# Plain float32 convolution for the first four tiles, and another order of the first steps

## The chip, the cores and the metric

The kernel runs on one NeuronCore of a Trainium2 chip. The metric is the device time of one execution in microseconds (us). The kernel before takes 187.44 us, the median of three runs (187.42 to 187.69).

The engines are named as the profile names them: PE is TensorE, PEld its weight load, DVE is VectorE, ACT is ScalarE, POOL is GpSimd and SP is SyncE, which here only issues transfers. SPq and ACTq are the instructions by which SP and ACT issue a transfer.

## The reference

```python
def cond(x, c, weight, c_weight, bias):          # x 128x32x512, 4 groups, 9 taps, padding 4
    out = lax.conv_general_dilated(x, weight, ..., feature_group_count=4)
    return out + einsum('nd,od->no', c, c_weight)[:, :, None] + bias[None, :, None]

def ffn(x, base_W, base_b, router_W, router_b, A, B, expert_map):   # x is cond's output
    base_out = x @ base_W.T + base_b                      # 512 -> 512
    probs = softmax(x @ router_W.T + router_b)            # 15 routes
    topk_p, topk_i = top_k(probs, 8)
    w = sum over k of topk_p * onehot(expert_map[topk_i]) # 8 experts
    h = einsum('btd,erd->bter', x, A)                     # 8 experts x 16
    lora = einsum('bter,eor->bto', h * w[..., None], B) * 2.0
    return base_out + lora

out = x + ffn(cond(x, ...))
```

## The kernel before, in words

**Tiles.** The 4096 rows (128 samples by 32 channels) of 512 positions are worked on as 32 tiles of 128 rows. A tile is 16 samples by the 8 channels of one convolution group. For each tile TensorE convolves (the positions are laid out in blocks so that a convolution is a product with 128x128 matrices, into `conv_banks`), VectorE adds the condition (`y_rows`) and transposes in 32x32 blocks (`y`), and TensorE multiplies `y` by one wide matrix, `wide_sb`, that holds A, the router and the base weights: 656 columns in two PSUM banks, the "front" bank of 400 columns and the "next" bank of 256, in four runs of 128 positions. From the front bank VectorE takes the router's scores, the eight best and the expert weights (`choose`, `best`, `mark`, `weigh`), and makes `hw`. TensorE turns `hw` (`turn_hw`) and multiplies it by B (`up`), into the same sums. VectorE adds them to the rows `xr`, and SP stores them.

**High and low parts.** A float32 operand is split in two float32r parts, a high one (ACT copies it with rounding: `wide_hi`, `y_hi`, `terms_hi`, `conv_hi`, `x_hi`, `hw_hi`) and a low one (the rest, by a subtraction on POOL or DVE: `..._lo`). Each product of the reference is then three float32r products: high by high, high by low, low by high.

**The first four tiles** are convolved from `x_in` directly: two matmuls (the group's own weights and those that reach into the next block) by three products, so six matmuls of 512 columns a tile, `conv_first` at line 566. Before them the input and the weights have to be split: `x_hi`, `x_lo`, `conv_hi`, `conv_lo`. Later tiles come from `terms`, prepared by an identity that saves a product: ACT copies one half of `terms` to PSUM (`odd_up`), DVE subtracts it (`difference`), ACT rounds (`terms_high`), POOL makes the rest (`terms_low`), and every second tile `edges` go through `edge`, `edge_high`, `edge_low`.

**Order.** There is no scheduler: each engine has its own program, written out by hand, and semaphores between them. TensorE starts with nine matmuls on zeros (`keep_warm`), convolves tiles 0 and 1, and then runs steps. Step t computes `linear(t)`'s front bank, `turn_hw(t-1)`, a part of the next bank, `up(t-1)`, the rest of the next bank, and the convolution of tile t+3. Steps 0 and 1 (`first_step`, `second_step`) have orders of their own, and convolve tiles 2 and 3. A step from 2 on starts when `y_lo` of its tile and the rows of tile t-2 (`out_added`) are there. `y_lo` is made by DVE for tiles 0 to 2 and by POOL from tile 3 on.

**Loads.** SP issues the transfers of the first tiles, of the wide matrix (four runs of 328 KB) and of most convolution weights, with a few waits between them; ACT issues the first two pieces of the convolution weights and the condition's inputs.

## Time and profile before

| what | us |
|---|---|
| median of three runs | 187.44 |
| profiled execution, its own time | 188.49 |
| profiled execution, span from first to last instruction | 186.7 |
| PE busy in the span | 180.1 (96%) |
| DVE busy | 156.2 (84%) |
| POOL busy | 143.9 (77%) |
| ACT busy | 82.9 (44%) |
| share of the chain that ended last on PE | 88% |

The mean granted TensorE clock is 0.997 of full speed. The profiled execution lies 1.05 us above the median, and 1.8 us of its time are outside the span. Share of the span says little of the first microseconds, where PE waits: the page's slices show PE at 7 and 8 tenths in the first three of 40 and 9 from then to the last. A line number names the line that records the instruction, which for the wide matmuls (L619), the convolution (L605, L566) and the subtractions (L217, L222) is a helper's.

### The profile page before, as it was taken

Reading aid. Unit: us, or ns where it says so; the run is one execution under the profiler, and the core shown is the slowest. Engines: PE = TensorE matmul, PEld = TensorE weight load, DVE = VectorE, ACT = ScalarE, POOL = GpSimd, SP = SyncE. Lnnn points to the kernel's source line nnn. Section 1 sums busy time; section 2 is a strip of 40 time slices with the busy share of each in tenths; the row PEclk is TensorE's granted clock in tenths of the full one; section 3 lists DMA queues with packets and bytes.
Section 4 is the critical chain, followed back from the end, with each engine's and each line's share of the span. In section 5 each row is a group of like instructions: output and inputs, shape, how many; then the busy total and the mean of one; then the engine's idle time right before and its main releaser. Section 6 shows DMA issues by size and latency. Waiting matters only on the chain.

```text
span 186.7 us, 3948 instructions
## 1 busy us (share of the span) xinstructions
PE 180.1 (96%) x1243; PEld 171.8 (92%) x1243; DVE 156.2 (84%) x513; ACT 82.9 (44%) x249; POOL 143.9 (77%) x141
## 2 busy tenths in 40 slices
PE   7889999999999999999999999999999999999992
PEld 2469979999999999999999999999999999999992
DVE  0997999989888888888888888889888889978673
ACT  3687344454343545444344545434354544422310
POOL 2639979988898888888988888879888887895410
PEclk9999999999999999999999999999999999999998
DMA  6999642755745454645555464754645631233313
GB/s 185 387 312 328 191 158 80 227 169 180 219 137 165 137 186 167 228 169 190 151 153 176 135 217 169 225 170 123 207 125 177 243 98 68 97 112 112 116 56 112
DMA packets 17733, 32.01 MB, mean 171 GB/s; under 512 B 1969, under 2 KB 2865, under 8 KB 17713
## 3 DMA queue, kind: packets, MB, share of 16 engines
q1 hardware_dynamic: 17136, 31.27, 51.9%
q10 hardware_dynamic: 576, 0.49, 0.9%
q8 instruction: 10, 0.16, 0.4%
q14 instruction: 11, 0.08, 0.1%
HBM read 23.36 MB, written 8.39 MB: 170 GB/s over the span
## 4 chain that ended last, share of the span: by engine, by line
PE 88%; DVE 4%; DMA 2%; issue 2%; ACT 2%; DVEq 0%; SPq 0%
PE wide_ps L619 58%; PE wide_ps L655 11%; PE conv_banks L605 10%; PE edge_bank L605 2%; DMA wide_sb<-wide_w 2%; PE odd_bank L642 2%; PE conv_banks L619 2%; PE conv_banks L566 2%; ACT wide_hi L350 1%; DVE xr L768 1%; DVE y_lo L887 1%; DVE y L859 0%; PE conv_banks L655 0%; DVE y_rows L774 0%; ACT y_hi L394 0%
## 5 line engine op out<-in xcount | busy, mean ns | idle before, releaser
L619 PE MATMUL wide_ps<-wide_hi,y_hi 128*128 128x400 f32 (+1 forms) x248 | 79.2, 325 | 1.3 <-ACT y_hi L394 0.7
L619 PE MATMUL wide_ps<-wide_hi,y_lo 128*128 128x400 f32 (+1 forms) x248 | 75.9, 312 | 0.0
L619 PE MATMUL wide_ps<-wide_lo,y_hi 128*128 128x400 f32 (+1 forms) x248 | 75.9, 312 | 0.0
L496 POOL TENSOR_TENSOR terms_lo<-terms,terms_hi 128x512 fp32r<-128x512 f32 x28 | 36.3, 1298 | 18.6 <-ACT terms_hi L379 18.5
L619 PEld LDWEIGHTS wide_ps<-wide_hi,y_hi 128*128 128x128 f32 x248 | 46.3, 188 | 3.9 <-ACT y_hi L394 1.1
L619 PEld LDWEIGHTS wide_ps<-wide_lo,y_hi 128*128 128x128 f32 x248 | 46.5, 189 | 0.0
L619 PEld LDWEIGHTS wide_ps<-wide_hi,y_lo 128*128 128x128 f32 x248 | 46.4, 188 | 0.0
L491 POOL TENSOR_TENSOR xr<-xr,base_b_sb 128x512 f32<-128x512 f32 x32 | 41.9, 1310 | 3.8 <-DMA xr<-x_rows 3.8
L514 POOL TENSOR_TENSOR y_lo<-y,y_hi 128x512 fp32r<-128x512 f32 x29 | 37.5, 1295 | 3.2 <-ACT y_hi L394 3.2
L401 ACT ACTIVATE hw_hi<-odd_bank 128x128 fp32r<-128x128 f32 x31 | 8.6, 277 | 52.7 <-PE odd_bank L642 52.7
L768 DVE TENSOR_TENSOR xr<-wide_ps,xr 128x512 f32<-128x512 f32 x30 | 20.7, 691 | 5.4 <-PE wide_ps L655 4.1
L859 DVE STREAM_TRANSPOSE y<-y_rows 128x512 f32<-128x512 f32 x32 | 22.8, 711 | 1.1
L394 ACT ACTIVATE y_hi<-y 128x512 fp32r<-128x512 f32 x32 | 20.0, 624 | 5.9 <-DVE y L859 4.9
L361 ACT ACTIVATE minus_best<-top 128x1 f32<-128x1 f32 x32 | 6.5, 203 | 32.6 <-DVE top L815 32.6
L379 ACT ACTIVATE terms_hi<-terms 128x512 fp32r<-128x512 f32 x28 | 17.3, 617 | 1.3 <-DVE terms L804 1.3
L605 PE MATMUL conv_banks<-terms_hi,conv_hi 128*128 128x256 f32 x56 | 15.7, 280 | 0.0
L605 PE MATMUL conv_banks<-terms_hi,conv_lo 128*128 128x256 f32 x56 | 15.7, 280 | 0.0
L605 PE MATMUL conv_banks<-terms_lo,conv_hi 128*128 128x256 f32 x56 | 15.6, 279 | 0.0
L842 DVE SCALAR_TENSOR_TENSOR hw<-wide_ps,inv,expert_w 128x128 f32<-128x128 f32 x31 | 10.9, 351 | 4.4
L655 PE MATMUL wide_ps<-up_hi,hw_lo 128*128 128x256 f32 x62 | 12.9, 286 | 0.0
L794 DVE TENSOR_TENSOR y_rows<-conv_banks,y_rows 128x256 f32<-128x256 f32 x28 | 11.9, 424 | 1.0
L797 DVE TENSOR_TENSOR y_rows<-edge_bank,y_rows 64x256 f32<-64x256 f32 x28 | 11.8, 422 | 1.0
(93 smaller groups left out, 321.3 us busy)
## 6 DMA issues: line engine op xcount, KB each, us to landing
xr<-x_rows SPq DMA_DIRECT2D x32, 256.0 KB, 3.6
out<-xr SPq DMA_DIRECT2D x31, 256.0 KB, 3.3
terms<-x_units SPq DMA_DIRECT2D x28, 256.0 KB, 3.0
edges<-x_edges SPq DMA_DIRECT2D x14, 256.0 KB, 3.5
wide_sb<-wide_w SPq DMA_DIRECT2D x4, 328.0 KB, 4.3
x_in<-x_first SPq DMA_DIRECT2D x4, 264.0 KB, 4.4
conv_sb<-conv_w SPq DMA_DIRECT2D x2, 192.0 KB, 5.0
conv_sb<-conv_w ACTq DMA_DIRECT2D x2, 128.0 KB, 4.5
```

The source lines that it names most:

```text
L379: nc.scalar.activation(terms_hi[i % 2][:, :, :, :], terms[i][:, :, :, :], ACT.Copy)\
L394: nc.scalar.activation(y_hi[k % 2][:, :, :], y[k % 2][:, :, :], ACT.Copy)\
L491: nc.gpsimd.tensor_tensor(xr[k][:, :], xr[k][:, :], base_b_sb[:, :], ALU.add)\
L496: nc.gpsimd.tensor_tensor(terms_lo[i % 2][:, :, :, :], terms[i][:, :, :, :], terms_hi[i % 2][:, :, :, :].bitcast(F32), ALU.subtract)\
L514: nc.gpsimd.tensor_tensor(y_lo[k % 2][:, :, :], y[k % 2][:, :, :], y_hi[k % 2][:, :, :].bitcast(F32), ALU.subtract)\
L605: mm = nc.tensor.matmul(sums, w[:, j, :], a[:, :, :], start=w is conv_hi and a is hi, stop=a is lo)
L619: mm = nc.tensor.matmul(sums_of(t, k)[:, b, 0:columns[1] - columns[0]], a[k % 2][:, r, :], w[:, r, columns[0]:columns[1]], start=r == 0 an ...
L655: mm = nc.tensor.matmul(sums_of(t, k)[:, b, first:first + HALF], a[k % 2][:, :], w[:, b * HALF:(b + 1) * HALF], start=False, stop=True, sk ...
L768: nc.vector.tensor_tensor(rows, linear_sums(t, k), rows, ALU.add)\
L794: nc.vector.tensor_tensor(rows[:, :, other, :], conv_ps[:, h, 1, :, :], rows[:, :, shared, :], ALU.add).then_inc(own_ready, 1)
L797: nc.vector.tensor_tensor(rows[reached, :, shared, :], edge_ps[reached], rows[reached, :, shared, :], ALU.add)\
L859: nc.vector.transpose(y[k % 2][:, :, :].rearrange("p r (n o) -> p n r o", n=Q), y_rows[k % 2][:, :, :, :].rearrange("p n a k -> p n (a k)"))\
```

## The change

The convolution of tiles 0 to 3 takes `x_in` and the loaded weights as they are, in float32, with two matmuls a tile instead of six. `x_hi` and `x_lo` are gone with their operations. The split convolution weights, used from tile 4 on, are kept in ten slots instead of fourteen, and the last pieces of them are split later (`conv_high(2)`, `conv_high(3)` in step 1). The condition's inputs and the convolution weights are one tensor, `conv_w`, loaded in pieces by columns. Tile 0's input is loaded and convolved in two halves. `y_hi` of tile 0 is made by DVE instead of ACT; `wide_lo` of run 0, `y_lo` of tile 2 and `up_lo` are made by POOL instead of DVE; the copies `cond_w_sb` by ACT instead of POOL. `up_lo` now reads a scaled copy `up_scaled`, made by ACT. The first `turn_hw` waits for the second `odd_up` instead of the first. The warm-up has six matmuls instead of nine. Steps 0 and 1 and the loads are in another order. The rest of the diff replaces `isinstance(t, int) and` by nothing, with the same program.

```diff
-WARM_UP = 9
+WARM_UP = 6
...
-            load_x(0)
+            for n, rows in enumerate(FIRST_ROWS):
+                load_first_x(n, rows)
+            load_x(1)
             load_wide(0)
-            load_x(1)
             load_wide(1)
-            sync.wait_ge(x_loaded[0], 16)
+            sync.wait_ge(x_first_in[1], 16)
             load_wide(2)
             load_wide(3)
             sync.wait_ge(wide_in[0], 16)
             load_conv(2)
             load_x(2)
             sync.wait_ge(wide_in[1], 16)
+            load_conv(3)
             load_x(3)
+            sync.wait_ge(wide_in[3], 16)
             load_terms(START, 0)
-            sync.wait_ge(wide_in[3], 16)
-            load_conv(3)
             load_edges(START // 2, 0)
...
+            act.wait_ge(cond_in, 16)
+            cond_weights(slice(0, 1))
+            cond_weights(slice(1, GROUPS))
+            bias_condition(range(1), 1)
             conv_high(0)
-            wide_high(range(1))
-            x_high(1)
-            bias_condition(0)
+            wide_high(range(RUNS))
+            bias_condition(range(1, 2), 2)
             conv_high(1)
-            wide_high(range(1, 2))
-            y_high(0, 0)
-            wide_high(range(2, RUNS))
-            conv_high(2)
-            x_high(2)
-            x_high(3)
+
+            y_high(1, 1, 2)
+            exponentials(0, 0)
+            bias_condition(range(2, GROUPS), 3)
             odd_up(START, 0)
-            y_high(1, 1)
-            conv_high(3)
-            bias_condition(1)
-            exponentials(0, 0)
             terms_high(START, 0)
             act.wait_ge(up_in, 16)
             nc.scalar.activation(up_hi[:, :], up_sb[:, :], ACT.Copy, scale=LORA_SCALE)\
                 .then_inc(up_hi_ready, 1)
+            nc.scalar.activation(up_scaled[:, :], up_sb[:, :], ACT.Copy, scale=LORA_SCALE)\
+                .then_inc(up_scaled_ready, 1)
             edge_high(START // 2, 0)
...
+            pool.wait_ge(wide_hi_ready, 1)
+            wide_low_part(nc.gpsimd, 0, wide_lo_first)
...
-            def conv_first_late(t):
-                pe.wait_ge(y_rows_ready, t - 1)
-                pe.wait_ge(conv_hi_ready, 3)
-                pe.wait_ge(x_hi_ready, t)
-                conv_first(t, (X_HIGH,))
-                pe.wait_ge(conv_lo_ready, 2)
-                conv_first(t, (X_W_REST,))
-                pe.wait_ge(x_lo_ready, t)
-                conv_first(t, (X_REST,)).then_inc(conv_done, 1)
+            def conv_first(t):
+
+
+
+                own, reach = t % 2, 1 - t % 2
+                nc.tensor.matmul(first_ps[:, t % 2, :, :], conv_sb[:, W_OWN[t], :],
+                                 x_in[t][:, :, own:own + BLK], start=True, stop=False)
+                nc.tensor.matmul(first_ps[:, t % 2, :, :], conv_sb[:, W_REACH[t], :],
+                                 x_in[t][:, :, reach:reach + BLK], start=False, stop=True)\
+                    .then_inc(conv_done, 1)
...
-                    pe.wait_ge(odd_ready, 1)
+                    pe.wait_ge(odd_ready, 2)
...
+            pe.wait_ge(conv_w_in[0], 16)
+            for n, rows in enumerate(FIRST_ROWS):
+                pe.wait_ge(x_first_in[n], 16)
+                for j, block in ((W_OWN[0], 0), (W_REACH[0], 1)):
+                    if n == 1 and block == 1:
+                        cond_sums(range(1), 1)
+                    mm = nc.tensor.matmul(first_ps[:, 0, rows, :], conv_sb[:, j, :],
+                                          x_in[0][:, rows, block:block + BLK],
+                                          start=j == W_OWN[0], stop=j == W_REACH[0])
+            mm.then_inc(conv_done, 1)
+            pe.wait_ge(conv_w_in[1], 16)
+            pe.wait_ge(x_loaded[1], 16)
+            conv_first(1)
+            cond_sums(range(1, 2), 2)
```

On POOL, the stretch from `terms_lo` of tile 4 (`terms_lo0<-terms0`, after the arrow what is read, with buffer numbers) to the split of the convolution weights reads before:

```order
L496 TENSOR_TENSOR terms_lo0<-terms0,terms_hi0 128x512 [waits terms_hi_ready]
L508 TENSOR_TENSOR edge_lo<-edges0,edge_hi 128x256 [waits edge_hi_ready]
L491 TENSOR_TENSOR xr0<-xr0,base_b_sb 128x512 [waits xr_loaded0,base_b_in]
L491 TENSOR_TENSOR xr1<-xr1,base_b_sb 128x512 [waits xr_loaded1]
L496 TENSOR_TENSOR terms_lo1<-terms1,terms_hi1 128x512 [waits terms_hi_ready]
L503 TENSOR_TENSOR edges1<-edges1 128x256 [waits edges_loaded1]
L514 TENSOR_TENSOR y_lo1<-y1,y_hi1 128x512 [waits y_hi_ready]
L222 TENSOR_TENSOR conv_lo<-conv_sb,conv_hi 128x384 [waits conv_hi_ready]
```

And now:

```order
L490 TENSOR_TENSOR terms_lo0<-terms0,terms_hi0 128x512 [waits terms_hi_ready]
L515 TENSOR_TENSOR up_lo<-up_scaled,up_hi 128x512 [waits up_hi_ready,up_scaled_ready]
L502 TENSOR_TENSOR edge_lo<-edges0,edge_hi 128x256 [waits edge_hi_ready]
L485 TENSOR_TENSOR xr0<-xr0,base_b_sb 128x512 [waits xr_loaded0,base_b_in]
L508 TENSOR_TENSOR y_lo0<-y0,y_hi0 128x512 [waits y_hi_ready]
L490 TENSOR_TENSOR terms_lo1<-terms1,terms_hi1 128x512 [waits terms_hi_ready]
L485 TENSOR_TENSOR xr1<-xr1,base_b_sb 128x512 [waits xr_loaded1]
L497 TENSOR_TENSOR edges1<-edges1 128x256 [waits edges_loaded1]
L508 TENSOR_TENSOR y_lo1<-y1,y_hi1 128x512 [waits y_hi_ready]
L479 TENSOR_TENSOR conv_lo<-weights_sb,conv_hi 128x256 [waits conv_hi_ready]
L479 TENSOR_TENSOR conv_lo<-weights_sb,conv_hi 128x384 [waits conv_hi_ready]
```

Three operations have come into the stretch (`up_lo`, `y_lo0` of tile 2, a `conv_lo` of 256 columns). Behind it both kernels go on alike: the rows of tile 2, `terms_lo` of tile 6, `edge_lo`, the rows of tile 3, and `y_lo` of tile 4.

On DVE, from the program's start to the weights of tile 0's experts (`hw0` follows the last row), before:

```order
L873 CAST x_hi0<-x_in0 128x528 [waits x_loaded0]
L222 TENSOR_TENSOR conv_lo<-conv_sb,conv_hi 128x256 [waits conv_hi_ready]
L217 TENSOR_TENSOR x_lo0<-x_in0,x_hi0 128x528 [waits x_hi_first]
L881 TENSOR_TENSOR wide_lo<-wide_sb,wide_hi 128x656 [waits wide_hi_ready]
L894 TENSOR_TENSOR is_expert<-cond_in_sb,expert_index 128x120 [waits index_ready,cond_in]
L774 TENSOR_TENSOR y_rows0<-conv_banks,cond_sb 128x512 [waits conv_done,cond_biased]
L859 STREAM_TRANSPOSE y0<-y_rows0 128x16x4x8 [waits y_rows_ready]
```

And now:

```order
L892 TENSOR_TENSOR is_expert<-weights_sb,expert_index 128x120 [waits index_ready,cond_in]
L779 TENSOR_TENSOR y_rows0<-conv_banks,cond_sb 128x512 [waits conv_done,cond_biased]
L864 STREAM_TRANSPOSE y0<-y_rows0 128x16x4x8 [waits y_rows_ready]
L900 CAST y_hi0<-y0 128x512 [waits y_ready]
L886 TENSOR_TENSOR y_lo0<-y0,y_hi0 128x512 [waits y_hi_first]
L226 TENSOR_TENSOR wide_lo<-wide_sb,wide_hi 128x656 [waits wide_hi_ready] x3
L779 TENSOR_TENSOR y_rows1<-conv_banks,cond_sb 128x512 [waits conv_done,cond_biased]
```

The splits of tile 0's input and of its weights are gone from in front of `y_rows0`, and the low parts of the wide matrix stand behind `y_lo0`. `difference` of tile 4 (`terms0<-terms0,odd_bank`) has moved too: it stood right behind the maximum of tile 0's scores, and stands now behind `hw0`.

On PE, from the first matmul after the warm-up to the first wide one, before:

```order
L566 MATMUL conv_banks<-x_hi0,conv_hi 128x512 [waits x_hi_first,conv_hi_ready]
L566 MATMUL conv_banks<-x_hi0,conv_hi 128x512
L566 MATMUL conv_banks<-x_hi0,conv_lo 128x512 [waits conv_lo_first]
L566 MATMUL conv_banks<-x_hi0,conv_lo 128x512
L628 MATMUL edge_bank<-cond_in_sb,cond_w_sb 128x128 [waits cond_w_ready,cond_in]
L628 MATMUL edge_bank<-cond_in_sb,cond_w_sb 128x128
L566 MATMUL conv_banks<-x_lo0,conv_hi 128x512 [waits x_lo_first]
```

And now:

```order
L666 MATMUL conv_banks<-x_in0,weights_sb 128x256 [waits x_first_in0,conv_w_in0]
L666 MATMUL conv_banks<-x_in0,weights_sb 128x256
L666 MATMUL conv_banks<-x_in0,weights_sb 128x256 [waits x_first_in1]
L624 MATMUL edge_bank<-weights_sb,cond_w_sb 128x128 [waits cond_in,cond_w_ready]
L666 MATMUL conv_banks<-x_in0,weights_sb 128x256
L566 MATMUL conv_banks<-x_in1,weights_sb 128x512 [waits x_loaded1,conv_w_in1]
L568 MATMUL conv_banks<-x_in1,weights_sb 128x512
L624 MATMUL edge_bank<-weights_sb,cond_w_sb 128x128 [waits cond_biased,cond_w_ready]
L609 MATMUL wide_ps0<-wide_hi,y_hi0 128x400 [waits wide_hi_ready,y_hi_first]
```

The first matmul waits only for transfers now, and not for DVE and ACT.

## Rows read from the trace of the kernel before

**Rows 1.** Stretches: busy time of each engine, PEclk, DMA share, GB/s.
```profile
30.00:170.00 140.00, 139.93 (x1009) 138.58 (x1010) 122.79 (x422) 62.34 (x195) 119.46 (x106) 1.00 0.51 163
```

**Rows 2.** Chain that ended last, 0 to 40 us: start, us, what.
```profile
14.82 0.45 PE edge_bank L628 x4
15.27 1.45 PE conv_banks L566 x6
...
20.33 0.12 PE odd_bank L642
...
24.05 2.42 PE wide_ps L619 x12
...
30.07 2.44 PE wide_ps L619 x12
...
35.97 2.19 PE wide_ps L619 x12
```

**Rows 3.** Timeline of PE: start, us, line, operation, [idle before, releaser].
```profile
0.99 3.88 PE L553 MATMUL wide_ps<-zeros 128*128 128x512 bf16 x9 [0.99 <-POOL zeros L459]
...
10.56 1.85 PE L619 MATMUL wide_ps<-wide_hi,y_hi 128*128 128x400 f32 x8 [0.67 <-ACT y_hi L394]
```

**Rows 4.** Timeline of DVE, first 18 us.
```profile
4.19 0.43 DVE L873 CAST x_hi<-x_in 128x528 fp32r<-128x528 f32 x1 [4.19 <-DMA x_in<-x_first]
...
6.11 1.08 DVE L881 TENSOR_TENSOR wide_lo<-wide_sb,wide_hi 128x656 fp32r<-128x656 f32 x1 [0.21 <-ACT wide_hi L350]
7.11 1.38 DVE L894 TENSOR_TENSOR is_expert<-cond_in_sb,expert_index 128x120 f32<-128x120 int32 x1
8.42 0.68 DVE L774 TENSOR_TENSOR y_rows<-conv_banks,cond_sb 128x512 f32<-128x512 f32 x1
9.13 0.71 DVE L859 STREAM_TRANSPOSE y<-y_rows 128x512 f32<-128x512 f32 x1
...
10.54 0.69 DVE L887 TENSOR_TENSOR y_lo<-y,y_hi 128x512 fp32r<-128x512 f32 x1
11.18 1.59 DVE L881 TENSOR_TENSOR wide_lo<-wide_sb,wide_hi 128x656 fp32r<-128x656 f32 x2
...
15.97 0.40 DVE L804 TENSOR_TENSOR terms<-terms,odd_bank 128x256 f32<-128x256 f32 x1
...
16.82 0.18 DVE L826 SCALAR_TENSOR_TENSOR wide_ps<-wide_ps,exps 128x15 f32<-128x15 f32 x1 [0.29 <-ACT exps L364]
...
17.75 0.35 DVE L842 SCALAR_TENSOR_TENSOR hw<-wide_ps,inv,expert_w 128x128 f32<-128x128 f32 x1
```

**Rows 5.** Groups by line, 0 to 32 us: shapes, count, busy us, mean ns, idle before.
```profile
L628 PE MATMUL edge_bank<-cond_in_sb,cond_w_sb 128*128 128x128 f32 x8 | 1.3, 284 | 0.2 <-POOL cond_w_sb L470 0.2
...
L605 PE MATMUL conv_banks<-terms_hi,conv_lo 128*128 128x256 f32 x4 | 1.1, 278 | 0.0
```

**Rows 6.** DMA, 0 to 25 us in 40 slices: GB/s moved.
```profile
GB/s 0 0 27 67 308 400 406 382 393 413 399 378 346 386 398 348 370 370 334 297 305 213 161 200 272 334 390 405 401 400 287 170 120 95 252 148 216 269 272 16
```

**Rows 7.** Timeline of ACT.
```profile
5.32 0.75 ACT L350 ACTIVATE wide_hi<-wide_sb 128x656 fp32r<-128x656 f32 x1 [0.50 <-DMA wide_sb<-wide_w]
...
16.63 0.61 ACT L379 ACTIVATE terms_hi<-terms 128x512 fp32r<-128x512 f32 x1
```

**Rows 8.** Timeline of POOL.
```profile
18.58 1.30 POOL L496 TENSOR_TENSOR terms_lo<-terms,terms_hi 128x512 fp32r<-128x512 f32 x1
...
27.24 1.28 POOL L514 TENSOR_TENSOR y_lo<-y,y_hi 128x512 fp32r<-128x512 f32 x1 [1.21 <-ACT y_hi L394]
28.48 1.03 POOL L222 TENSOR_TENSOR conv_lo<-conv_sb,conv_hi 128x384 fp32r<-128x384 f32 x1
29.45 1.30 POOL L491 TENSOR_TENSOR xr<-xr,base_b_sb 128x512 f32<-128x512 f32 x1
...
31.95 0.75 POOL L508 TENSOR_TENSOR edge_lo<-edges,edge_hi 128x256 fp32r<-128x256 f32 x1
...
33.88 1.32 POOL L514 TENSOR_TENSOR y_lo<-y,y_hi 128x512 fp32r<-128x512 f32 x1
```

More of the change, by code:

```diff
@@ L210, in from_tile, with wide_low_part @@
         def from_tile(t, least):
[L211 removed]
+            return t >= least
         def up_to_tile(t, most):
[L214 to L217 removed]
+            return t <= most
+        def wide_low_part(ops, r, ready):
+            ops.tensor_tensor(wide_lo[:, r, :], wide_sb[:, r, :], wide_hi[:, r, :].bitcast(F32),
                               ALU.subtract).then_inc(ready, 1)
[L220 to L223 removed]
         def sums_of(t, k):
[L228 removed]
+            if t >= TILES - 2:
                 return conv_banks[:, :, :] if t == TILES - 2 else wide_ps[0][:, :, :]
@@ L232, in hwt_of @@
         def hwt_of(t):
-            return edge_bank[:, 0:P] if isinstance(t, int) and t == TILES - 1 else hwt_ps
+            return edge_bank[:, 0:P] if t == TILES - 1 else hwt_ps
         def linear_sums(t, k):
@@ L334, in _, with cond_weights @@
             nc.scalar.activation(zero_exp[:, :], zeros[:, 0:1], ACT.Exp)
+            def cond_weights(groups):
+                nc.scalar.copy(cond_w_sb[:, groups, :, :],
+                               cond_w_in_sb[:, groups, :].unsqueeze(2)
+                               .to_broadcast([P, groups.stop - groups.start, BP, CG]))\
+                    .then_inc(cond_w_ready, 1)
             def conv_high(piece):
-                own = W_PIECES[piece]
-                act.wait_ge(conv_w_in[piece], 16)
-                nc.scalar.activation(conv_hi[:, own, :], conv_sb[:, own, :], ACT.Copy)\
+                split, own, loads = S_PIECES[piece]
+                for load in loads:
+                    act.wait_ge(conv_w_in[load], 16)
+                nc.scalar.activation(conv_hi[:, split, :], conv_sb[:, own, :], ACT.Copy)\
                     .then_inc(conv_hi_ready, 1)
-            def x_high(i):
-                act.wait_ge(x_loaded[i], 16)
-                nc.scalar.activation(x_hi[i][:, :, :], x_in[i][:, :, :], ACT.Copy)\
-                    .then_inc(x_hi_ready, 1)
             def wide_high(runs):
@@ L516, in y_low, with up_low @@
                     .then_inc(y_lo_ready, tiles)
+            def up_low():
+                pool.wait_ge(up_scaled_ready, 1)
+                pool.wait_ge(up_hi_ready, 1)
+                nc.gpsimd.tensor_tensor(up_lo[:, :], up_scaled[:, :], up_hi[:, :].bitcast(F32),
+                                        ALU.subtract).then_inc(up_lo_ready, 1)
+            conv_low(0)
+            conv_low(1)
             edge(START // 2, 0)
-            conv_low_later(3)
             def step(t, k, p, q):
-                if isinstance(t, int) and t == 0:
+                if t == 0:
                     terms_low(t + 4, k)
+                    up_low()
                     edge_low(p + 2, k // 2)
@@ L624, in linear, with cond_sums @@
                 return mm
-            def cond_sums(groups):
+            def cond_sums(groups, copies):
+                pe.wait_ge(cond_w_ready, copies)
+                if groups.start > 0:
+                    pe.wait_ge(cond_biased, groups.start)
+                if groups.start == 0:
+                    pe.wait_ge(cond_in, 16)
                 for g in groups:
@@ L915, in _ @@
             weigh(0, 0)
+            difference(START, 0)
             dve.wait_ge(cond_biased, GROUPS)
             def step(t, k, p, q):
-                if isinstance(t, int) and t == 0:
+                if t == 0:
                     condition_first(2)
```

270 lines of the change are left out of this document (115 added, 155 removed).

## The prediction, made before the changed kernel was timed

> **What bounds the kernel now.** I read the stretches first. From 30 to 170 us PE is busy for 139.93 of 140.00 us [rows 1]: nothing that the change touches lies there, and as long as the work of a step stays the same, the end comes as much earlier as PE gets into that stream. So the question is when PE begins a step behind which it no longer waits. I then read the chain of waits for the first 40 us: the step for tile 4 begins at 35.97 us [rows 2], and before it the steps for tiles 2 and 3 begin at 24.05 and 30.07 [rows 2], 6.02 and 5.90 us long. Last I read the timelines of the engines for what PE waits for before that: it spends 0.99 to 4.88 us on nine warm-up matmuls, and its first wide matmul starts at 10.56 after a wait for `y_hi` [rows 3]. The start of step 4 is the number to predict.
>
> **The convolution in float32.** Three products in float32r are replaced by one in float32. Six matmuls of 512 columns take 1.45 us, so 0.24 us each [rows 2]. The only float32 matmuls of the trace that are no transposes are those of the condition: two for tiles 2 and 3, recorded as four instructions, take 0.45 us [rows 2], 0.11 us for 128 columns, and two instructions to a matmul. That spacing is an upper end for the cost per column, since it may be the weight load that sets it. The lower end is the float32r one: 2 instructions of 0.24 us, 0.48 us for 512 columns. The upper is 2 x 4 x 0.11 = 0.90. I take 0.86: the instruction of 128 float32 columns shows 284 ns and that of 256 float32r columns 278 [rows 5], as if a float32 column took twice the time, so 2 instructions x 2 x 512 columns at 2.4 GHz. A tile then costs 1.71 us of PE instead of 1.45, +0.26 a tile (ends -0.5 and +0.35). For tiles 2 and 3 this is +0.5 of PE work between 8 and 20 us; for tiles 0 and 1 it is in the chain to the first `y`.
>
> The trace shows two instructions for such a matmul [rows 2]. The Trainium skill (FP8 and Floating Point Precision, TensorE Precision Notes) says that true float32 is four passes through the array; that would be four column times against three for the split products, and agrees with the 0.86 us that I take and speaks against this part of the change taken alone.
>
> **The start.** Before, tile 0 needs x (landed at 4.19 [rows 4]), the cast, the splits, six matmuls and a DVE that is busy with `wide_lo` and `is_expert` until 8.49; `y_rows` starts at 8.42, the transpose ends at 9.84, ACT's `y_hi` follows, and PE starts at 10.56 [rows 3, 4]. Now: half of x and the first weights are 260 KB instead of 392; at about 390 GB/s [rows 6] that is 0.3 us less, and I take 4.1 for the first matmul (between 3.8 and 4.6). Four half matmuls of 0.43 us and the condition's 0.22 end at 6.1. `is_expert` (1.38 us) begins when the condition's inputs land, which I put at 4.7, so DVE is free at 6.1 too. Then `y_rows` 0.68, transpose 0.71, `y_hi` as a DVE cast 0.43 [rows 4]: `y` is there at 7.6 instead of 9.84 and `y_hi` at 8.1. PE's convolution of tile 1 (1.71 us) fills the time to 8.0. The wide runs: run 0 landed at 5.32 before [rows 7]; x of tile 1 and one weight piece (392 KB) now go ahead of it, +1.0 us, so its high part (0.75 us) is there at 7.1; the other three come at 0.8 us each, since as many bytes precede them as before. That is in time for a start at 8.1.
>
> **DVE from there.** `y_lo` 0.69, three `wide_lo` at 0.80 each (1.59 for two) are done at 11.2. I add 0.4: the one `wide_lo` that ran beside POOL's copies took 1.08 us against 0.80 for those that did not [rows 4], and POOL now subtracts its own `wide_lo` and a `conv_lo` here. So 11.6; `y_rows` and the transpose of tile 1 end at 13.0, ACT's `y_hi` takes 0.6 (as `terms_hi`, of the same shape [rows 7]), `y_lo` 0.69, then the expert weights, 16.82 to 18.10 before, 1.28 us [rows 4], with some 0.25 allowed for `mark` in front: 15.9. Only then comes `difference` (0.40 us), which stood at 15.97 before [rows 4], and `terms_hi` of tile 4 ends at 16.9 on ACT instead of 17.24 [rows 7]. So of the 2.2 us by which `y` is earlier, 0.3 is left here: the move of `difference` costs the rest.
>
> The row for that contention is the 1.08 against 0.80 us [rows 4]. The Trainium skill (GPSIMD Engine Reference, the table of its first section) says that GpSimd shares its SBUF interfaces with VectorE and contends with those of its instructions that read two SBUF inputs; this agrees with the row. By it `up_lo` and `y_lo` of tile 2, moved from DVE to POOL, also spare DVE two such instructions between 19 and 23 us.
>
> **PE between.** First wide matmul 8.1. It can't finish before the last `wide_lo` (11.6), so step 0's products end at 12.2 (before at 14.82, where the condition's begin [rows 2]). Condition 0.45, tile 2 1.71, front bank of tile 1 2.2 (the 12 matmuls of 2.19 [rows 2]), tile 3 1.71: 18.3. There `turn_hw` waits for the second `odd_up`. On ACT that stands behind `terms_hi` (16.9), `up_hi`, the new `up_scaled` (0.55 each, by the 0.61 of the same shape), `edge_hi`, `y_hi` and itself: 19.3. So PE stands for 1.0 us and goes on at 19.3 against 20.33 [rows 2]. The rest of step 1 took 3.72 us with its waits (20.33 to 24.05), I take 3.3. Step 2 then starts at 22.6. Steps 2 and 3 took 6.02 and 5.90; the products alone are 2.19 for the front bank [rows 2], 0.12 for the turn, and 24 matmuls of 256 columns at 0.12 (of the 0.24 for 512), so 5.2, or 5.55 with the edges of every second step. I take 5.3 and 5.6 since `hw`, `y_lo` and the rows are early now. PE by itself would be at step 4 at 33.5, 2.5 us earlier than before.
>
> **POOL.** This is what is late next. Step 4 waits for `y_lo` of tile 4, the end of a line of POOL work that begins with `terms_lo` of tile 4. Before, it ran from 18.58 to 35.20 [rows 8], 0.8 us ahead of PE, which began at 35.97. In the new program this line holds eleven operations of 512 columns at a spacing of 1.25 (two from 29.45 to 31.95), three of 256 columns on edges and one on weights at 0.72 (31.95 with 0.75), and one of 384 at 1.0 [rows 8]: 13.75 + 2.9 + 1.0 = 17.65, and 0.07 for the end of the last. It begins at 16.9: 34.6. That is 1.1 later than PE, so PE waits there, and step 4 starts at 34.65 instead of 35.97, -1.3 us. Behind it POOL needs four operations, 4.45 us, to the next `y_lo`, and PE 5.2: it doesn't wait again. Bounds: if DVE's neighbours slow POOL as between 18.58 and 28.48 (9.9 us less 1.21 idle [rows 8], for what sums to 7.7 at these spacings) it is 35.6, -0.4; if POOL isn't slowed and the chain to `terms_hi` is 0.9 us quicker (the lower float32 cost on two tiles), PE decides, at -2.5.
>
> **The sum.** 188.49 - 1.3 = 187.2 for the execution of the profile, which lies 1.05 above the median: 187.44 - 1.3 = 186.1 us. Everything else is free: six fewer subtractions on POOL and ACT before 17 us, where both then idle; the later split of the last weights (ACT, after 21 us); the order of loads behind the wide runs, which PE doesn't reach before 12 us.
>
> **Rivals.**
> *PE decides (185.0).* POOL's line fits in, because it is shorter or starts earlier, and the gain is the 2.5 us of PE: 184.9 to 185.3. For it: POOL's durations are rough; against it: it would have to be 1.1 us shorter than its rows say.
> *The clock comes late (187.9).* The nine warm-up matmuls run at 0.43 us, which for 512 columns is 1.2 GHz; the six of [rows 2] at 0.24 us are at 2.4 GHz. PE had worked without a gap from 0.99 to 4.88 before the fast ones [rows 3]. Now the warm-up ends at 3.6 and PE stands until 4.1. If the rise comes only after tile 0, its four half matmuls and the condition cost 3.9 us instead of 1.95, all of it in the chain to `y`, `terms_hi` and POOL's line: 34.6 + 1.9 = 36.5, 0.5 later than before. It decides from a delay of 1.3 us on. For it: less work in front than the trace shows before the rise; against: a half-microsecond gap is small, and PE is busy again behind it. The Trainium skill (TensorE: Matmul & The Clock Gate, Part 1) says that the array starts throttled and that only sustained activity releases it; the trace agrees in that its first nine are slow, and by that rule fewer of them and a gap are a risk.
> *Nothing is left (187.4).* The chain through DVE is a further microsecond late (the condition's inputs land at 5.5, the contention is dearer) and POOL's line ends where it did: within 0.3 of before.
>
> **Chances.** Forecast, 185.6 to 186.9: 0.50. PE decides: 0.18. Clock: 0.17. Nothing left: 0.15. The forecast's and the first rival's cases are faster, some of the last too: faster by over 0.2% 0.68, within 0.2% (0.37 us, about what runs of this kernel can tell) 0.14, slower 0.18. The range takes in most of the clock's case and the upper part of "PE decides": 184.9 to 187.8.
>
> **What would show it.** In the profile after: first convolution matmul at 3.8 to 4.6, instructions of 256 float32 columns at 0.21 us apart (0.43 if the clock is late, 0.12 if the float32 cost is the lower); `y` at 7.6; first wide matmul at 8.1; PE's `turn_hw` of tile 0 released by ACT's `odd_bank` near 19.3; POOL without idle time from 16.9 to 34.6, and PE waiting about 1 us for POOL's `y_lo` at step 4. It is wrong if PE doesn't wait for POOL between 25 and 36 us, or if step 4 begins after 35.6.

## The result and the profile after

The changed kernel takes 189.10 us (median of 9 runs, 188.66 to 189.69), the kernel before 187.69 in the same session (9 runs, 187.22 to 188.24). The ratio is 1.0066, 95% interval 1.0050 to 1.0082: slower by 0.7%, where 1.3 us less were forecast. The profiled execution took 189.29 us, its span is 187.5 (before 188.49 and 186.7), the mean granted clock 0.997 in both.

I read it in the order of the prediction. The stream first, as busy time by stretch (us, then PE, PEld, DVE, ACT, POOL with their instruction counts, clock, DMA share, GB/s):

```profile
0.00:10.00 10.00, 7.83 (x23) 4.24 (x23) 3.23 (x5) 5.44 (x10) 3.07 (x17) 1.00 0.82 266
...
20.00:40.00 20.00, 18.42 (x129) 17.54 (x129) 15.54 (x51) 9.21 (x28) 19.96 (x20) 1.00 0.47 156
42.00:170.00 128.00, 128.00 (x928) 126.84 (x927) 112.25 (x385) 56.75 (x178) 108.53 (x97) 1.00 0.50 162
```

From 42 us on PE is busy all the time, as before [rows 1]; between 20 and 40 us it misses 1.6 us while POOL is busy for 19.96 of 20. So the comparison is again when step 4 begins. The chain that ended last (start, us, what), from the split of the last weights to there:

```profile
29.19 1.42 POOL conv_lo L479 x2
...
35.07 1.24 POOL y_lo L508
36.31 0.14 issue
36.45 2.44 PE wide_ps L609 x12
...
41.83 2.19 PE wide_ps L609 x12
```

Before, the same view had:

```profile
35.62 0.35 PE edge_bank L605 x3
35.97 2.19 PE wide_ps L619 x12
...
41.10 2.19 PE wide_ps L619 x12
```

The last piece ahead of step 4 was PE's own work, and the step began at 35.97. Now it is POOL's `y_lo` of tile 4, and the step begins at 36.45. Its first twelve products take 2.44 us instead of 2.19, so step 5 begins at 41.83 instead of 41.10. That 0.73 stays to the end, and the span is 0.8 longer.

The 2.44 needs a word, since it comes back in the experiments. PE's timeline has the first two products of step 4, before and now:

```profile
35.81 0.34 PE L619 MATMUL wide_ps<-wide_hi,y_hi 128*128 128x400 f32 x1
35.99 0.34 PE L619 MATMUL wide_ps<-wide_lo,y_hi 128*128 128x400 f32 x1
```

```profile
36.45 0.42 PE L609 MATMUL wide_ps<-wide_hi,y_hi 128*128 128x400 f32 x1 [0.80 <-POOL y_lo L508]
36.70 0.34 PE L609 MATMUL wide_ps<-wide_lo,y_hi 128*128 128x400 f32 x1
```

A product of 0.34 us starts 0.18 us behind the one in front, so it overlaps it by 0.16. The chain counts a group without a wait from the end of the product in front, 35.97, though its own first product started at 35.81; behind a wait it counts from the first product. So 0.16 of the 0.25 is overlap that the wait has taken away, and 0.08 is the second product, which follows the first by 0.25 instead of 0.18. From start to start, step 4 is 0.64 us late, and with that 0.08 step 5 is as late as the chain says, within 0.01. A wait costs PE a quarter of a microsecond more than the idle time listed with it; the other products of the group are as quick as ever.

The timelines (start, us, engine, line, operation, xcount, idle before and its releaser) show how the start got there. PE:

```profile
0.99 2.74 PE L557 MATMUL wide_ps<-zeros 128*128 128x512 bf16 x6 [0.99 <-POOL zeros L465]
3.71 2.48 PE L666 MATMUL conv_banks<-x_in,weights_sb 128*128 128x256 f32 x6
6.24 0.60 PE L666 MATMUL conv_banks<-x_in,weights_sb 128*128 128x256 f32 x2
14.57 1.02 PE L566 MATMUL conv_banks<-x_in,weights_sb 128*128 128x512 f32 x2
15.43 1.02 PE L568 MATMUL conv_banks<-x_in,weights_sb 128*128 128x512 f32 x2
21.15 0.33 PE L638 MATMUL odd_bank<-ident,hw 128*128 128x128 f32 x1 [0.78 <-ACT odd_bank L383]
```

DVE:

```profile
4.32 0.28 DVE L892 TENSOR_TENSOR is_expert<-weights_sb,expert_index 128x120 f32<-128x120 int32 x1 [4.32 <-DMA weights_sb<-conv_w]
8.42 1.48 DVE L900 CAST y_hi<-y 128x512 fp32r<-128x512 f32 x1
9.94 1.01 DVE L886 TENSOR_TENSOR y_lo<-y,y_hi 128x512 fp32r<-128x512 f32 x1
10.87 2.33 DVE L226 TENSOR_TENSOR wide_lo<-wide_sb,wide_hi 128x656 fp32r<-128x656 f32 x3
15.31 1.08 DVE L886 TENSOR_TENSOR y_lo<-y,y_hi 128x512 fp32r<-128x512 f32 x1 [0.49 <-ACT y_hi L404]
17.88 0.41 DVE L809 TENSOR_TENSOR terms<-terms,odd_bank 128x256 f32<-128x256 f32 x1
```

ACT's high part of tile 4, and POOL:

```profile
18.32 0.63 ACT L389 ACTIVATE terms_hi<-terms 128x512 fp32r<-128x512 f32 x1 [1.74 <-DVE terms L809]
```

```profile
8.04 1.58 POOL L226 TENSOR_TENSOR wide_lo<-wide_sb,wide_hi 128x656 fp32r<-128x656 f32 x1 [6.17 <-ACT wide_hi L360]
9.58 0.82 POOL L479 TENSOR_TENSOR conv_lo<-weights_sb,conv_hi 128x256 fp32r<-128x256 f32 x1
15.12 0.73 POOL L497 TENSOR_TENSOR edges<-edges 128x256 f32<-128x256 f32 x1 [0.53 <-DMA edges<-x_edges]
19.03 1.27 POOL L490 TENSOR_TENSOR terms_lo<-terms,terms_hi 128x512 fp32r<-128x512 f32 x1 [3.19 <-ACT terms_hi L389]
```

`y` of tile 0 is there at 8.38 instead of 9.84 [rows 4], a gain of 1.5 us. But `terms_hi` ends at 18.95 instead of 17.24 [rows 7], a loss of 1.7, and POOL, which before had old work until 18.58 [rows 8], stood idle for 3.19 us ahead of `terms_lo`. From there it works without a gap to 36.30. Of the two signs that the prediction gave for being wrong, one is seen: PE does wait for POOL, but step 4 begins after 35.6. And PE's `turn_hw` of tile 0, released by `odd_bank` as forecast, comes at 21.15 instead of 19.3.

### The profile page after: what moved, and what is told of

Read it like the earlier page. It is cut to its first block, busy times and chain, and to the rows that moved or that the text cites. A ratio compares the mean times of both kernels' runs of the same rounds, so it can differ in the third digit from the quotient of the medians.

```text
span 187.5 us, 3930 instructions
## 1 busy us (share of the span) xinstructions
PE 180.0 (96%) x1236; PEld 171.7 (92%) x1236; DVE 152.4 (81%) x508; ACT 81.4 (43%) x247; POOL 140.6 (75%) x139
## 4 chain that ended last, share of the span: by engine, by line
PE 80%; POOL 8%; DVE 7%; issue 2%; ACT 1%; DVEq 0%; POOLq 0%; ACTq 0%
PE wide_ps L609 51%; PE wide_ps L651 10%; PE conv_banks L595 9%; POOL xr L485 3%; PE edge_bank L595 2%; POOL y_lo L508 2%; PE odd_bank L638 2%; PE conv_banks L609 2%; PE conv_banks L666 2%; PE wide_ps L557 1%; POOL terms_lo L490 1%; DVE wide_lo L226 1%; DVE y_lo L886 1%; DVE y_hi L900 1%; DVE y L864 1%
## 5 line engine op out<-in xcount | busy, mean ns | idle before, releaser
L508 POOL TENSOR_TENSOR y_lo<-y,y_hi 128x512 fp32r<-128x512 f32 x30 | 38.9, 1296 | 2.1 <-ACT y_hi L404 2.1
L404 ACT ACTIVATE y_hi<-y 128x512 fp32r<-128x512 f32 x31 | 19.4, 627 | 2.0 <-DVE y L864 1.0
```

The lines of the kernel that those rows point to most:

```text
L404: nc.scalar.activation(y_hi[k % 2][:, :, :], y[k % 2][:, :, :], ACT.Copy)\
L508: nc.gpsimd.tensor_tensor(y_lo[k % 2][:, :, :], y[k % 2][:, :, :], y_hi[k % 2][:, :, :].bitcast(F32), ALU.subtract)\
```

## The experiments

Theory 1 of the expectations: `terms_hi` of tile 4 is late because DVE is slowed beside POOL and because `difference` stands at the end of DVE's line; POOL's line then passes this on to step 4. Theory 2: PE's time in the float32 convolution (its columns, or its clock) is what was lost. Theory 3 came later and is told in its place. Each run is timed in five rounds against the kernel before on the same chip; the changed kernel's own ratio, 1.0066, measured in the same way in its own session, is the mark to compare with.

**`difference` back in its place.** `best(0, 0)` is followed by the difference again, and on ACT `odd_up` and `terms_high` stand ahead of what they waited behind:

```diff
+            odd_up(START, 0)
             y_high(1, 1, 2)
             exponentials(0, 0)
-            bias_condition(range(2, GROUPS), 3)
-            odd_up(START, 0)
             terms_high(START, 0)
+            bias_condition(range(2, GROUPS), 3)
...
             best(0, 0)
+            difference(START, 0)
...
             weigh(0, 0)
-            difference(START, 0)
```

> In the changed kernel the difference of tile 4 on DVE stands again right behind the maximum of tile 0's scores, and odd_up and terms_high of tile 4 on ACT stand ahead of what they then wait behind. Theory 1 (POOL's line decides by its start): terms_hi of tile 4 starts at 15.3 to 16 instead of 18.32, POOL's line begins some 2.5 us earlier, PE no longer waits for y_lo at step 4 and starts it at 35.0 to 35.7 instead of 36.45; the time falls by 0.8 to 1.4 us. Theory 2 (PE's own work and waits before step 4 decide): the time stays within 0.2 us, since no work of PE is changed.

Measured: 187.19 us (11 runs), ratio 0.9964 [0.9947, 0.9982], so 1.9 us less than the changed kernel by the difference of the ratios, and faster than both kernels. Its timelines (ACT; POOL; then DVE), and PE's chain:

```profile
15.47 0.61 ACT L389 ACTIVATE terms_hi<-terms 128x512 fp32r<-128x512 f32 x1
```

```profile
16.16 1.30 POOL L490 TENSOR_TENSOR terms_lo<-terms,terms_hi 128x512 fp32r<-128x512 f32 x1 [1.08 <-ACT terms_hi L389]
...
32.45 1.29 POOL L508 TENSOR_TENSOR y_lo<-y,y_hi 128x512 fp32r<-128x512 f32 x1
```

```profile
8.19 1.48 DVE L900 CAST y_hi<-y 128x512 fp32r<-128x512 f32 x1
14.51 0.40 DVE L809 TENSOR_TENSOR terms<-terms,odd_bank 128x256 f32<-128x256 f32 x1
```

```profile
34.37 2.20 PE wide_ps L609 x12
```

The start is as slow as in the changed kernel (the cast takes the same 1.48 us), and yet step 4 begins at 34.37: POOL's line starts 2.9 us earlier and ends at 33.74, 0.6 ahead of PE. The place of one DVE operation of 0.40 us and of the two ACT operations around it decides between a gain and a loss; what either engine's order is worth by itself wasn't run. The gain over the changed kernel is larger than the 0.8 to 1.4 us expected, and step 4 earlier than the 35.0 to 35.7.

**The same move in the kernel before.** Only `difference` goes behind the expert weights there, with a wait of PE's first turn for it:

```diff
             best(0, 0)
-            difference(START, 0)
...
             weigh(0, 0)
+            difference(START, 0)
...
+                if not from_tile(t, 1):
+                    pe.wait_ge(differences_ready, 1)
```

> The kernel before with one edit of the change alone: VectorE's difference of tile 4 comes behind the expert weights of tile 0 (a wait on TensorE's turn of tile 0 for it is added, which should cost nothing). Theory 1 (the move of difference costs only where GpSimd has nothing else to do): difference moves from 15.97 to about 17.7, terms_hi of tile 4 from 16.63 to about 18.1, and GpSimd, which was busy with older work until 18.6, begins terms_lo at 18.7 to 18.9 instead of 18.58; 0.8 us of slack before step 4 takes that up: time within 0.2% of before. Theory 3 (the move costs its 1.7 us wherever it stands): step 4 starts about 1 us later, ratio 1.004 to 1.006.

Measured: ratio 1.0011 [0.9996, 1.0026]. ACT and POOL:

```profile
18.27 0.63 ACT L379 ACTIVATE terms_hi<-terms 128x512 fp32r<-128x512 f32 x1 [1.74 <-DVE terms L806]
```

```profile
18.97 1.30 POOL L496 TENSOR_TENSOR terms_lo<-terms,terms_hi 128x512 fp32r<-128x512 f32 x1 [0.55 <-ACT terms_hi L379]
```

`terms_hi` is as late as in the changed kernel, 1.64 us later than before, and it costs no measurable time (the interval leaves room for 0.5 us): POOL was at older work until 18.4, and the 0.4 us by which its line starts later are taken from its wait at 27 us, 0.89 us now and 1.21 before [rows 8]; `y_lo` of tile 4 begins at 33.85, before at 33.88 [rows 8]. So theory 3 falls: a late `difference` costs time where POOL's older work is gone and three operations have come into its line, and next to nothing where that isn't so. The two edits aren't quite each other's reverse, since this one leaves ACT's `odd_up` where it was.

**One POOL operation more, in both kernels.** `spare` is 512 columns wide, and the added subtraction (1.05 us) stands in step 1:

```diff
+                    nc.gpsimd.tensor_tensor(spare[:, :], base_b_sb[:, :], base_b_sb[:, :], ALU.subtract)
```

> The changed kernel with one more POOL operation of 512 columns (a subtraction whose result nobody reads) behind the split of the last weights in step 1. Theory 1 (POOL's line decides): all of it, 1.25 us, is seen at step 4 (37.7 instead of 36.45) and the time rises by 1.0 to 1.3 us. Theory 2 (PE or DVE decides): POOL has the idle time, and the time rises by less than 0.3 us.

> The kernel before with one GpSimd subtraction of 512 columns more, in the same place as in extraA. Theory 1: GpSimd's line to y_lo of tile 4 had about 0.8 us of slack before step 4 in this kernel, so of its 1.05 us only 0.2 to 0.45 us reach the end: ratio 1.000 to 1.0025, step 4 at 36.1 to 36.4 with a short wait for y_lo. Rival (an operation more on GpSimd costs its full length in either kernel, by contention or otherwise): +1.0 us as in extraA, ratio 1.0055.

Measured, changed kernel: 190.00 us, ratio 1.0120 [1.0097, 1.0142], 0.54% above 1.0066, the whole 1.0 us. PE:

```profile
37.49 0.43 PE L611 MATMUL wide_ps<-wide_hi,y_hi 128*128 128x400 f32 x1 [1.81 <-POOL y_lo L509]
```

Its wait grew from 0.80 to 1.81 us. So POOL's line is what step 4 waits for. Kernel before: ratio 1.0046 [1.0028, 1.0063], +0.86 us and not the 0.2 to 0.45 expected. Its PE timeline and chain:

```profile
35.45 0.45 PE L621 MATMUL wide_ps<-wide_hi,y_hi 128*128 128x400 f32 x1 [0.28 <-POOL y_lo L515]
```

```profile
35.45 2.46 PE wide_ps L621 x12
40.85 2.44 PE wide_ps L621 x12
46.58 2.19 PE wide_ps L621 x12
```

The wait itself is the expected size, 0.28 us. But the product group behind it takes 2.46 instead of 2.19, and the next one at 40.85 takes 2.44; that one begins as soon as POOL's next `y_lo` (39.47 to 40.78) is there: POOL had stood 0.88 us for the transfer of `xr`. 0.28 + 0.27 + 0.25 is 0.80, about what the runs show. Slack is used up earlier than its size says, since each short wait also costs PE the quarter of a microsecond told above.

**POOL's `wide_lo` kept away from the cast.**

```diff
             pool.wait_ge(wide_hi_ready, 1)
+            pool.wait_ge(y_hi_first, 1)
             wide_low_part(nc.gpsimd, 0, wide_lo_first)
```

> One wait more than in the changed kernel: POOL begins wide_lo of run 0 only when DVE's cast y_hi of tile 0 is done. Theory 1 (POOL's line from terms_lo of tile 4 to y_lo of tile 4 decides, and its late start comes in good part from the cast, 1.48 us beside POOL's subtraction instead of 0.43): the cast takes 0.43 us, terms_hi of tile 4 starts 0.7 to 1.05 us earlier than 18.32, step 4 starts at 35.5 to 35.8 instead of 36.45, and the time falls by 0.6 to 1.0 us. Theory 2 (the cast is slow by itself, or POOL's line is not what decides and the loss is PE's own float32 work): the cast stays at 1.48, or it falls to 0.43 and the time stays within 0.2 us.

Measured: 189.16 us, ratio 1.0068 [1.0043, 1.0092], no gain. DVE and POOL (of an execution 0.8 us above its median):

```profile
8.32 0.43 DVE L901 CAST y_hi<-y 128x512 fp32r<-128x512 f32 x1
9.39 4.87 DVE L226 TENSOR_TENSOR wide_lo<-wide_sb,wide_hi 128x656 fp32r<-128x656 f32 x3
```

```profile
8.90 2.03 POOL L226 TENSOR_TENSOR wide_lo<-wide_sb,wide_hi 128x656 fp32r<-128x656 f32 x1 [7.03 <-DVE y_hi L901]
10.90 1.24 POOL L480 TENSOR_TENSOR conv_lo<-weights_sb,conv_hi 128x256 fp32r<-128x256 f32 x1
```

The cause of the slow cast is shown: without POOL beside it, it takes 0.43 us. But the contention only moved: three `wide_lo` take 4.87 us instead of 2.33, and POOL's own operations 2.03 and 1.24 instead of 1.58 and 0.82. Theory 1 was right on the cast and wrong on what removing it this way brings.

The slow casts of all the traces tell more of how it comes about. POOL's `wide_lo` has begun before each of them (ends and starts in us):

| trace | POOL's `wide_lo` ends | cast starts | from there to that end | cast takes |
|---|---|---|---|---|
| changed kernel | 9.62 | 8.42 | 1.20 | 1.48 |
| `difference` back in its place | 9.39 | 8.19 | 1.20 | 1.48 |
| split of the weights moved (below) | 9.46 | 8.20 | 1.26 | 1.55 |
| warm-up of eight (below) | 9.62 | 8.32 | 1.30 | 1.57 |
| one POOL operation more | 10.07 | 8.61 | 1.46 | 1.75 |

The cast ends 0.27 to 0.29 us behind POOL's operation every time. It isn't slower by a factor: by these rows it stands until the operation that POOL began first is over. What it costs is what is left of POOL's operation at that moment, so a long operation on POOL is dear to whatever short one on DVE begins just behind it.

**`wide_lo` of run 0 on DVE**, so that POOL has nothing beside the cast:

```diff
-            pool.wait_ge(wide_hi_ready, 1)
-            wide_low_part(nc.gpsimd, 0, wide_lo_first)
...
             y_low(0, 0)
+            dve.wait_ge(wide_hi_ready, 1)
+            wide_low_part(nc.vector, 0, wide_lo_first)
             wide_low(1)
```

> In the changed kernel wide_lo of run 0 is made by DVE again, behind y_lo of tile 0, so POOL has nothing beside DVE's cast and subtractions between 8 and 12.8 us. Theory 1 (the neighbours on POOL cost DVE time; each DVE operation with POOL at work takes longer): the cast takes 0.43 us instead of 1.48, y_lo 0.69 instead of 1.01, four wide_lo 0.80 each, and DVE is through with them at 12.7 instead of 13.2, although it has one operation more; terms_hi of tile 4 starts 0.4 to 0.5 us earlier, step 4 as well, and the time falls by 0.3 to 0.5 us against the changed kernel. Theory 2 (the neighbours don't matter): DVE is through at 14.0, and the time rises by 0.8.

Measured: 188.40 us (12 runs), ratio 1.0031 [1.0012, 1.0050], 0.35% or 0.7 us below the changed kernel, where 0.3 to 0.5 were expected; the two intervals just touch. One more operation on DVE is cheaper than the same one on POOL beside it: the cast takes 0.43, `y_lo` 0.69, and all four `wide_lo`

```profile
8.56 3.09 DVE L226 TENSOR_TENSOR wide_lo<-wide_sb,wide_hi 128x656 fp32r<-128x656 f32 x4
```

The profiled execution was the quickest of the twelve, 187.4, so its step 4 (34.48, behind a wait of 0.63 for `y_lo`) isn't compared. It shows something else, PE at tile 0:

```profile
3.52 1.73 PE L664 MATMUL conv_banks<-x_in,weights_sb 128*128 128x256 f32 x6
```

Six instructions in 1.73 us, where the changed kernel's took 2.48, from the same warm-up and nearly the same start: from execution to execution PE reaches the spacing of 2.4 GHz before or behind them. Of the seven traces with this start and six warm-up matmuls it is the only quick one; the others have 2.35 to 2.74.

**The clock.** A warm-up of eight matmuls instead of six:

```diff
-WARM_UP = 6
+WARM_UP = 8
```

> The changed kernel with eight warm-up matmuls instead of six. In the changed kernel the first six float32 instructions of tile 0 took 0.41 us each and the last two 0.22. Theory 1a (the clock rises as in the kernel before, with PE at work without a gap until about 4.4 us): tile 0's eight instructions all take 0.21 to 0.22 us, the first starts at 4.45 instead of 3.71, tile 0 is done at 6.4 instead of 6.85, the time falls by 0.3 to 0.5 us. Theory 1b (the clock rises at 6.0 us whatever stands before): tile 0 ends 0.3 us later and the time rises by 0.3 us.

Measured: 189.26 us, ratio 1.0065 [1.0042, 1.0087], no change. PE:

```profile
4.38 1.71 PE L666 MATMUL conv_banks<-x_in,weights_sb 128*128 128x256 f32 x6
```

The first six instructions are faster now (0.29 us each against 0.41), but begin 0.67 us later, and tile 0 is done at the same time within 0.1 us. So neither 1a nor 1b holds. The slow clock costs the changed kernel some 0.7 us at the start (2.48 against the 1.73 above), and two more warm-up matmuls don't give it back. Whether they made the six instructions quick isn't shown: it is one trace, and one with six warm-up matmuls had the same.

**Float32 alone.** The kernel before, with the convolution of tiles 0 to 3 in float32 and the splits of their input left out (all splits of weights stay):

```diff
-                for product in products:
-                    w, a = product
-                    for j, blocks in ((W_OWN[t], t % 2), (W_REACH[t], 1 - t % 2)):
...
+                for j, blocks in ((W_OWN[t], t % 2), (W_REACH[t], 1 - t % 2)):
+                    mm = nc.tensor.matmul(first_ps[:, t % 2, :, :], conv_sb[:, j, :],
+                                          x_in[t][:, :, blocks:blocks + BLK],
...
```

> The kernel before with one part of the change alone: tiles 0 to 3 are convolved in float32 with two matmuls, and the splits of their input are left out; order, loads, nine warm-up matmuls and all splits of weights as before. Theory 1 (float32 columns cost four passes: 0.86 us for 512 columns as in the changed kernel's trace, so 1.71 instead of 1.43 a tile, +0.5 us for tiles 2 and 3 on PE, against a y of tile 0 that is there 0.5 us earlier, and a POOL freed of three subtractions of 1.3 us): between -0.4 and +0.3 us. Theory 2 (plain float32 is what made the changed kernel slower): +0.8 us or more.

Measured: 188.40 us (12 runs), ratio 1.0028 [1.0009, 1.0048], so 0.5 us more, between 0.2 and 0.9, with no wait for POOL at step 4. That lies above the range of theory 1 and below that of theory 2. It is a cost, of the size of the 0.26 us a tile on tiles 2 and 3, and not the whole 1.2 us. Since `difference` back in its place turns the loss into a gain with the float32 convolution left in, theory 2 falls as the main cause.

**The late split of the weights.** `conv_low(2)` (256 of the 640 columns that take 1.42 us at 29.19 in POOL's line above) is moved to where POOL was idle, and `conv_high(2)` on ACT with it:

```diff
             conv_high(1)
+            conv_high(2)
...
-                    conv_high(2)
                     conv_high(3)
...
             edge(START // 2, 0)
+            conv_low(2)
...
-                    conv_low(2)
                     conv_low(3)
```

> In the changed kernel the split of convolution weights piece 2 (ACT and POOL, 256 columns) is moved from step 1 into the idle time that ACT has before 14.6 us and POOL has between 15.9 and 19.0 us. Theory 1 (POOL's line decides by its length): the line is 0.72 us shorter, step 4 starts at 35.7 to 35.8 instead of 36.45, the time falls by 0.5 to 0.75 us. Theory 2 (POOL's line does not decide): no work is removed, and the time stays within 0.2 us.

Measured: 188.72 us (12 runs), ratio 1.0034 [1.0017, 1.0051], 0.3% or 0.6 us less, as expected by theory 1. Step 4 begins at 35.55, 0.9 us earlier: 0.6 by the shorter line, 0.3 because this execution's line began at 18.72 instead of 19.03. It still begins behind a wait of 0.25, and behind it POOL, now early, stands 0.92 us for the transfer of `xr`:

```profile
35.55 2.43 PE wide_ps L609 x12
40.95 2.44 PE wide_ps L609 x12
46.67 2.20 PE wide_ps L609 x12
```

The first two groups come behind waits, and of 0.9 us 0.64 are left at 46.67 (47.31 in the changed kernel). The program did on POOL at 29 us what it could have done at 15.

**Both repairs together**: `difference` in its old place and run 0's `wide_lo` on DVE.

> The changed kernel with the difference of tile 4 in its old place and wide_lo of run 0 on DVE. Theory 1 (with the difference early POOL's line no longer decides, PE does, from its first wide matmul on): the first wide matmul starts at 8.9 instead of 9.7 (diff alone), PE has no wait behind 13 us, step 4 starts 0.3 to 0.7 us earlier than 34.37, and the time is 0.3 to 0.7 us under that of diff alone, about 1.3 us under the kernel before. Theory 2 (DVE's chain to hw of tile 0 or POOL decides): within 0.2 us of diff alone.

Measured: 187.05 us (12 runs), ratio 0.9956 [0.9938, 0.9974]. It is the lowest ratio of all, but only 0.15 us under that of `difference` alone, which its interval holds: the further 0.3 to 0.7 us that were expected aren't seen. Nor are they in the trace, where step 4 begins at 34.31 against 34.37. PE's first wide matmul comes at 8.85 instead of 9.73, and PE waits nowhere for POOL, but it stands 0.33 us for `wide_lo` at 12.59 and 0.33 for ACT's `odd_bank` at 19.86, and that `odd_bank` stands behind DVE's work for tiles 0 to 2, in which `y_lo` of tile 1 takes 1.02 us beside POOL's `edges` (0.69 in the trace of `difference` alone). That is theory 2's case. `terms_hi` began only 0.13 us earlier than there, so what an earlier one would be worth isn't tested.

## Why the prediction was wrong, step by step

Right: that the start of step 4 is the number; that POOL's line from `terms_lo` to `y_lo` of tile 4 takes the place of PE's work there; its length, 17.65 forecast and 17.27 measured (19.03 to 36.30), for the most part because the two last splits of weights took 1.42 us and not 1.72; the float32 price, 0.86 us for 512 columns (14.57 to 15.43); that the move of `difference` eats the gain at `y`. That both the text and the runs say 1.9 us there is chance: in the text it is 2.2 less 0.3, time at `terms_hi`; in the runs it is the whole kernel's time, and `terms_hi` moved by 2.85 (18.32 to 15.47).

The step that failed first, and cost most, is "`terms_hi` of tile 4 ends at 16.9". It ended at 18.95, 2.05 us later, and the sum is its parts:

| part | forecast | measured | late by |
|---|---|---|---|
| convolution of tile 0 done | 6.1 | 6.84 | 0.74 |
| from there to `y` | 1.5 | 1.54 | 0.04 |
| from `y` to `y_hi` | 0.5 | 1.52 | 1.02 |
| `y_lo` and three `wide_lo` | 3.5 | 3.30 | -0.20 |
| rows and transpose of tile 1 | 1.4 | 1.35 | -0.05 |
| `y_hi`, `y_lo`, expert weights | 2.9 | 3.41 | 0.51 |
| `difference`, `terms_hi` | 1.0 | 0.99 | 0.0 |

The largest term is the cast. I took 0.43 us for it, measured where POOL was idle [rows 4], and allowed 0.4 for contention behind it, at `wide_lo`, from the row of 1.08 against 0.80. The contention fell on the cast, and was 1.05 us. Rows with its true size were there. `is_expert`, 120 columns, took 1.38 us [rows 4]; I read that as the operation's own length, but it takes 0.28 alone, and in the kernel before POOL had begun a subtraction 0.08 us ahead of it:

```profile
7.03 1.32 POOL L217 TENSOR_TENSOR x_lo<-x_in,x_hi 128x528 fp32r<-128x528 f32 x1 [0.53 <-ACT x_hi L344]
```

And `y_lo` of tile 2, 0.69 us alone, took 1.83 there beside POOL's additions, the first of which had begun 0.02 us ahead of it:

```profile
21.00 1.83 DVE L887 TENSOR_TENSOR y_lo<-y,y_hi 128x512 fp32r<-128x512 f32 x1
```

```profile
20.98 2.99 POOL L491 TENSOR_TENSOR xr<-xr,base_b_sb 128x512 f32<-128x512 f32 x2
```

The Trainium skill (GPSIMD Engine Reference, 1. Specifications) names, beside the two-input instructions that I cited, those of VectorE in a 2-port mode, and VectorE: DVE Perf Modes (Mode 2×_2P) says that copies of one float32 tensor in SBUF can run so; the cast is such a copy, and the trace agrees that it contends, 0.43 against 1.48. I had used half of the rule.

The convolution's 0.74 is a smaller form of the rival on the clock: six of the eight float32 instructions at 0.41 us instead of 0.22, 1.1 us, less the 0.4 by which the first began ahead of the forecast 4.1. It had been priced at up to 1.95 and given 0.17. The 0.51 is mostly `y_lo` of tile 1, 1.08 beside POOL's `edges` instead of 0.69.

From there the prediction's arithmetic holds: 2.05 later at `terms_hi`, 0.38 given back by POOL's shorter line, 0.13 in gaps, so step 4 at 34.65 + 1.8 = 36.45. What it lacked was the price of waiting, 0.25 us beside the idle time. Instead of -1.3 against the profile of before, that makes +0.48 at step 4 in the chain's count and +0.73 at step 5.

A second step failed, the last of the sum. It took 1.3 off the median, 187.44, as well as off the profiled execution, 188.49, and so carried the 1.05 us by which that execution was late over to the changed kernel. There the profiled execution was only 0.19 above its median. So of the 3.0 us between 186.1 and 189.10, 1.8 are the start of step 4, 0.25 the price of waiting, and 0.86 this step; it is also why the runs show a loss of 1.2 to 1.4 us and the two profiles 0.8.

What made the profiled execution of before late can be seen in part. In the kernel before with one POOL operation more, the program is the same until 28 us, and there DVE and POOL had:

```profile
6.98 0.27 DVE L896 TENSOR_TENSOR is_expert<-cond_in_sb,expert_index 128x120 f32<-128x120 int32 x1
```

```profile
7.13 1.31 POOL L218 TENSOR_TENSOR x_lo<-x_in,x_hi 128x528 fp32r<-128x528 f32 x1 [0.77 <-ACT x_hi L345]
```

Here `is_expert` began ahead of POOL's subtraction and took 0.27 us instead of 1.38; `y_rows` starts at 7.59 instead of 8.42 [rows 4], and `terms_hi` at 15.82 instead of 16.63 [rows 7]. Two tenths of a microsecond in when they begin are worth 0.8 us to the kernel before, and the changed kernel, whose `is_expert` has no POOL operation beside it, has no such pair. How often the executions of before fall on either side isn't on record, so this is not shown to be the whole of the difference.

Of the rivals, "nothing is left" had the right mechanism, POOL's line made late by dearer contention, and priced that at a microsecond. Together with the clock's part it was two, and the range didn't hold the sum of both.

Not tried: the split products kept for tiles 2 and 3 alone, which by the 0.26 us a tile would give PE half a microsecond beside `difference` in its old place.

## What to carry to other kernels

When a change lets one engine begin earlier, ask for each operation on the way which engine now runs beside it, and take its duration from a row with the same neighbour; a short operation that looks too long in the trace is that row. Where an operation stands until its neighbour is over, a long neighbour that begins a moment earlier costs up to its whole length, so look at which of the two begins first. Before a forecast for the median is made from one profile, ask what made that execution late, and whether the change leaves it in. Before moving an operation back on its engine, look at what the engine after next is doing at that moment: a result that is late for an idle engine with a long line behind it costs all of its delay, one that is late for an engine busy with older work little or nothing. And slack isn't free to its last tenth: add to each wait on TensorE the overlap that the next product loses by it.
